# A routed FFN whose tiles are ordered by their rows, with the picks of a token group loaded once a counted number of tiles is scattered

## What is computed

```python
x = _layernorm(x + _L0_attn_ref(x, ...), axis=-1)
x = _layernorm(x + _L0_ffn_ref(x, ...), axis=-1)
```

```python
logits = flat @ router_w.T
probs = jax.nn.softmax(logits.astype(jnp.float32), axis=-1)
topk_p, topk_i = jax.lax.top_k(probs, TOP_K)              # TOP_K = 2, E = 8
topk_w = (topk_p / jnp.maximum(topk_p.sum(-1, keepdims=True), 1e-09)).astype(flat.dtype)
...
for e in range(E):
    out = out + _mlp(flat, w_fc[e], w_proj[e]) * combine[:, e:e + 1]
out = out + _mlp(flat, shared_fc, shared_proj)            # _mlp: square(relu(x @ w_fc.T)) @ w_proj.T
```

## Time and profile before, and how to read it

| | |
|---|---|
| median of 3 runs | 490.98 us (490.75 to 491.0) |
| span of the profiled execution | 498.7 us |
| busy PE, DVE, ACT, POOL | 453.9, 356.7, 354.5, 315.1 us |
| granted TensorE clock, mean | 0.974 |
| first routed load to last `ob` | 327.14 to 470.4 us |
| first pick load to the end | 473.41 to 498.7 us |

### The profile page before, as it was taken

One profiled execution on the slowest core, in us unless ns is written; L12 is line 12 of the kernel. 1 busy time (PEld: TensorE's weight loads), 2 busy tenths in 40 slices (PEclk: granted clock), 3 DMA queues, 4 the chain that ended last, 5 costly groups with the idle time before them and its releaser, 6 DMA issues.

```text
span 498.7 us, 7644 instructions
## 1 busy us (share of the span) xinstructions
PE 453.9 (91%) x2184; PEld 293.6 (59%) x2184; DVE 356.7 (72%) x873; ACT 354.5 (71%) x557; POOL 315.1 (63%) x285
## 2 busy tenths in 40 slices
PE   8997999999999988798898898489999999999983
PEld 5332444444344333455576675389999999899721
DVE  5898999999999999998688964353333333455246
ACT  3989999999999999815455555327667667566537
POOL 4754789999999999845566666604555455555421
PEclk9998999999999999989799999979999999999997
DMA  8031246654343434001111111131222222222095
GB/s 274 8 122 43 86 146 213 216 196 151 130 153 131 151 133 148 3 1 33 39 45 43 45 43 47 46 94 51 72 65 81 71 60 58 60 57 67 11 324 182
DMA packets 41193, 48.56 MB, mean 97 GB/s; under 512 B 5616, under 2 KB 25266, under 8 KB 41152
## 3 DMA queue, kind: packets, MB, share of 16 engines
q1 hardware_dynamic: 35792, 39.07, 23.8%
q0 software_dynamic: 5216, 8.70, 5.6%
q10 hardware_dynamic: 144, 0.31, 0.2%
HBM read 19.17 MB, written 29.11 MB: 97 GB/s over the span
## 4 chain that ended last, share of the span: by engine, by line
PE 40%; POOL 22%; DVE 16%; issue 8%; ACT 7%; DMA 2%; another core or an unknown queue 2%; DVEq 0%; POOLq 0%; SPq 0%; ACTq 0%
POOL memory_feat L495 17%; PE routed_ph L1500 13%; PE routed_po L1513 12%; PE dispatch_sph L998 4%; PE dispatch_spo L1008 3%; POOL memory_feat L503 2%; DVE memory_prod L769 2%; DVE memory_y_raw L778 2%; POOL memory_prod L518 2%; PE memory_nsum L620 1%; ACT finish_xo L1714 1%; PE routed_px L1488 1%; PE dispatch_plr L969 1%; DVE memory_feat L769 1%
## 5 line engine op out<-in xcount | busy, mean ns | idle before, releaser
L495 POOL TENSOR_TENSOR memory_feat<-memory_feat,memory_p_tok 128x1024 f32<-128x1024 f32 x64 | 125.9, 2063 | 17.1 <-ACT memory_feat L390 14.2
L620 PE MATMUL memory_nsum<-memory_feat,tri 128*128 128x512 f32 x256 | 118.1, 604 | 6.3 <-ACT memory_last_rows L403 2.4
L1476 POOL DMA_INDIRECT pick_scratch<-routed_ob,routed_xg x71 | 71.6, 1008 | 75.1 <-DVE routed_ob L1597 56.7
L1192 POOL DMA_INDIRECT table_scratch<-dispatch_xrow,dispatch_slot x64 | 61.9, 967 | 40.9 <-PE dispatch_sph L998 18.9
L620 PEld LDWEIGHTS memory_nsum<-memory_feat,tri 128*128 128x128 f32 x256 | 47.8, 192 | 65.1 <-issue 56.2
L1546 ACT ACTIVATE routed_rel<-routed_ph 128x512 f32<-128x512 f32 x71 | 42.3, 597 | 47.7 <-PE routed_ph L1500 46.7
L1513 PE MATMUL routed_po<-routed_w2c,routed_hid 128*128 128x128 f32 x568 | 71.3, 276 | 1.2 <-DVE routed_ob L1597 0.7
L1500 PE MATMUL routed_ph<-routed_xs,routed_w1c 128*128 128x256 f32 (+1 forms) x368 | 71.1, 337 | 1.2 <-DVE routed_w2c L1583 0.9
L1597 DVE TENSOR_SCALAR routed_ob<-routed_po,routed_xg 128x128 f32<-128x128 f32 x71 | 22.6, 347 | 69.2 <-issue 49.6
L769 DVE TENSOR_TENSOR memory_prod<-memory_nsum,memory_query 128x1024 f32<-128x1024 f32 x58 | 68.8, 1216 | 1.9 <-PE memory_nsum L620 1.8
L1513 PEld LDWEIGHTS routed_po<-routed_w2c,routed_hid 128*128 128x128 f32 x568 | 67.0, 192 | 1.9 <-issue 1.1
(11 more groups left out here) (192 smaller groups left out, 694.6 us busy)
## 6 DMA issues: line engine op xcount, KB each, us to landing
table_scratch<-memory_blank SPq DMA_DIRECT2D x68, 260.0 KB, 2.6
finish_pick<-pick_scratch SPq DMA_DIRECT2D x16, 256.0 KB, 6.0
routed_xg<-table_scratch SPq DMA_DIRECT2D x25, 130.0 KB
w<-w_up SPq DMA_DIRECT2D x9, 256.0 KB, 2.7
w<-w_down SPq DMA_DIRECT2D x9, 256.0 KB, 3.1
x_tok<-x SPq DMA_DIRECT2D x4, 512.0 KB, 3.7
out<-finish_xo SPq DMA_DIRECT2D x7, 256.0 KB, 2.3
routed_xg<-table_scratch SPq DMA_DIRECT2D x21, 65.0 KB
```

The costliest lines, as they stand in the source:

```text
L495: nc.gpsimd.tensor_tensor(v, v, pv, ALU.mult).then_inc(wfeat_done, 1)
L620: last = nc.tensor.matmul(nsum[:, o:o + 512], tri[:], feat[:, i % U, h, q * 512:(q + 1) * 512], start=True, stop=True)
L1192: nc.gpsimd.indirect_dma_start(out=table, in_=xrow[:, r, n, :], in_offset=None, out_offset=bass.IndirectOffsetOnAxis(ap=slot[:, r, n:n + 1 ...
L1476: nc.gpsimd.indirect_dma_start(out=pick_dram, in_=ob[:, u, h, :], in_offset=None, out_offset=bass.IndirectOffsetOnAxis(ap=xg[:, t % XU, h, ...
```

## The change

Five things change.

The order of the routed tiles: candidates are (block k, expert e), k outermost, so all experts' first blocks come first. Partition p = 8 k + e of the chip stands for one candidate, and the list is worked out by small matrix products: `totals` sums the counts of every group (not only the last), DVE marks the candidates that are full (`valid`), PE numbers them with the triangular matrix (`order`), DVE makes a one-hot of the number (`pick_tiles`), PE turns that into lists of experts and starts (`tiles`), and DVE copies them (`list_tiles`); `bases` counts each expert's taken blocks, and the halves go the same way. The numbers of tiles, 25 and 21, stay.

The count: a candidate is needed by a group if the expert's rows up to that group reach into it. `reach` has the tile's number where that is so, PE turns it (`turn_reach`), DVE takes the largest (`far`), and `settle[g]` is that plus 4.

The loads: SP waits no longer for the last scatters but, for each group, for `kept` to reach `settle[g]`, which it loads into a register. As tile t is kept only after the scatter of tile t - 4 has landed, that stands for the scatters of all tiles the group needs. For the last four, POOL raises `kept` when their scatters have landed (`tick`).

The buffers: `pick`, `xo` and the small arrays of `finish` lie where `xrow` and `x_tok` were, or are made earlier (`Late`).

The order on PE in `finish`: `shared(0)` and `shared(1)` come before the routed stage, the rest between the `picks`. The banks are dealt out anew (`BANKS`).

```diff
-        self.seen = sb("seen", [P, 2, E], F32R)
+        self.seen = sb("seen", [P, NG + 1, E], F32R)
...
+class Late:
+    def __init__(self, nc, c, xrow, x_tok):
+        self.pick = xrow[:].rearrange("p r t c -> p (r t c)")[:, 0:2 * NT * D].rearrange("p (r t d) -> p r t d", r=2, t=NT)
...
-            def total():
+            def totals():
                 pe.wait_ge(seen_done, NG + 1)
                 pe.wait_ge(slot_done, NG)
-                nc.tensor.matmul(pr[:, GT * E:], ones_r[:], seen[:, NG % 2], start=True, stop=True).then_inc(total_done, 1)
+                nc.tensor.matmul(p_sum, ones_r[:], seen[:, 1:NG + 1].rearrange("p g e -> p (g e)"), start=True, stop=True
+                                 ).then_inc(total_done, 1)
+            def order(kind):
+                pe.wait_ge(valid_done, kind + 1)
+                nc.tensor.matmul(p_pos[:, kind:kind + 1], tri[:], valid[:, kind:kind + 1], start=True, stop=True
+                                 ).then_inc(order_done, 1)
+            def tiles(kind):
+                pe.wait_ge(chosen_done, kind + 1)
...
+                nc.tensor.matmul(p_tile[:, a:a + n], pair_e, chosen[:, kind, 0:n], start=True, stop=True)
+                nc.tensor.matmul(p_tile[:, TILES + a:TILES + a + n], origin[:] if kind else full_row, chosen[:, kind, 0:n],
+                                 start=True, stop=True).then_inc(tiles_done, 1)
+            def bases():
+                pe.wait_ge(taken_done, 1)
+                nc.tensor.matmul(p_pos[:, 2:3], alike, taken[:], start=True, stop=True).then_inc(base_done, 1)
+            def turn_reach():
+                pe.wait_ge(reach_done, 1)
+                nc.tensor.transpose(p_reach, reach[:, 0], ident[:]).then_inc(reach_turned, 1)
...
+                up(NG - 1, 0)
+                totals()
+                up(NG - 1, 1)
+                down(NG - 2, 0)
+                order(0)
+                down(NG - 2, 1)
+                tiles(0)
+                up(NG - 1, 2)
+                bases()
+                down(NG - 2, 2)
+                order(1)
+                up(NG - 1, 3)
+                tiles(1)
+                down(NG - 2, 3)
+                turn_reach()
                 for t in range(GT):
                     down(NG - 1, t)
...
+            def settle_groups():
+                dve.wait_ge(reach_turned, 1)
+                link(nc.vector.tensor_reduce(far[:], p_reach, AX.X, ALU.max))
+                nc.vector.tensor_scalar(settle[:], far[:], float(U), None, ALU.add).then_inc(settled, 1)
...
                 table_of_tiles()
+                table_of_halves()
                 add_shared(NG - 2)
-                table_of_halves()
+                settle_groups()
                 add_shared(NG - 1)
...
         def sync(sp):
-            for scattered, count in rou.scattered:
-                sp.wait_ge(scattered, count)
+            sp.wait_ge(dis.settled, 1)
             def load(g):
+                tiles = sp.value_load(settle[g:g + 1, 0:1], min_val=U + 1, max_val=TILES + U)
+                sp.wait_ge(rou.kept, tiles)
                 for r in range(2):
...
+        def early_tensor(pe):
+            pe.wait_ge(dis.added, NG - 1)
+            shared(0)
+            pe.wait_ge(dis.settled, 1)
+            shared(1)
...
-            shared(4)
-            shared(7)
-            pe.wait_ge(rou.x_kept, TILES)
-            shared(6)
-            pe.wait_ge(rou.rel_done, rou.banks)
-            for g in range(4):
-                shared(g)
-            pe.wait_ge(rou.kept, TILES)
-            shared(5)
             for n in range(len(PARTS)):
                 if n == 5:
                     pe.wait_ge(act_done, 1)
                     shared(NG)
                 picks(n)
+                if n == 0:
+                    pe.wait_ge(rou.x_kept, TILES)
+                    shared(2)
+                    pe.wait_ge(rou.rel_done, rou.banks)
+                if n + 3 == NG - 1:
+                    pe.wait_ge(rou.kept, TILES)
+                if n + 3 < NG:
+                    shared(n + 3)
...
         def gpsimd(pool):
+            for n, (scattered, count) in enumerate(rou.scattered):
+                pool.wait_ge(scattered, count)
+                nc.gpsimd.memset(tick[:, n:n + 1], 0.0).then_inc(rou.kept, 1)
```

More of the change, by code:

```diff
@@ L91, in build @@
         dis = dispatch(nc, c, early, mem, x_tok, y_all, ident, tri, rows, w_out, routerT, w_up, w_down, w1, w2,
-                       expert, start, table)
+                       expert, start, settle, table)
+        late = Late(nc, c, early.xrow, x_tok)
         rou = routed(nc, c, dis, ident, w1, w2, expert, start, table, pick_dram)
-        fin = finish(nc, c, rou, ident, y_all, eps, warm, pick_dram, out)
+        fin = finish(nc, c, late, dis, rou, ident, y_all, eps, warm, settle, pick_dram, out)
         block = c.enter_context(nc.Block())
@@ L853, in dispatch @@
 def dispatch(nc, outer, early, mem, x_tok, y_all, ident, tri, rows, w_out, routerT, w_up, w_down, w1, w2,
-             expert, start, table):
-    MOST = REGION // ROWS
+             expert, start, settle, table):
     LAST_REDUCES = {2: NT - 2, 3: NT - 1}
@@ L872, in dispatch @@
         ratio, hot, sel, part, seen, base = early.ratio, early.hot, early.sel, early.part, early.seen, early.base
-        hit, spot, slot, steps, fills = early.hit, early.spot, early.slot, early.steps, early.fills
-        one8, whole, used, left, halves = early.one8, early.whole, early.used, early.left, early.halves
-        stride, base0, past, owner, moved = early.stride, early.base0, early.past, early.owner, early.moved
+        hit, spot, slot, mine, total = early.hit, early.spot, early.slot, early.mine, early.total
+        valid, seq, taken, seat = early.valid, early.seq, early.taken, early.seat
+        edge, origin, chosen, reach, far = early.edge, early.origin, early.chosen, early.reach, early.far
         bits = early.bits
@@ L920, in dispatch @@
         token = rows[:, P:P + NT]
+        pair = rows[:, P + NT:]
+        own, full_end, full_at = pair[:, 0:E], pair[:, E:E + 1], pair[:, E + 1:E + 2]
+        pair_e, full_row, half_at, half_row = [pair[:, E + n:E + n + 1] for n in range(2, 6)]
+        alike = pair[:, E + 6:]
         def group(g):
@@ L1050, in rest @@
                 down(0, 3)
-                for g in range(2, NG):
+                for g in range(2, NG - 1):
                     if g + 2 < NG:
@@ L1302, in table_of_tiles, with list_tiles @@
+            def list_tiles(kind):
+                dve.wait_ge(tiles_done, kind + 1)
+                v = slice(FULL, TILES) if kind else slice(0, FULL)
+                nc.vector.tensor_copy(expert[:, v], p_tile[:, v])
+                nc.vector.tensor_scalar(start[:, v], p_tile[:, TILES + v.start:TILES + v.stop], float(P), float(EMPTY),
+                                        ALU.mult, ALU.add).then_inc(tabled, 1)
             def table_of_tiles():
                 dve.wait_ge(total_done, 1)
-                n_e = pr[:, GT * E:]
@@ L1809 @@
     pos = np.arange(L)
[L1810 removed]
+    tabs = np.zeros((P, 2 * P + P + NT + NPAIR), np.float32)
     tabs[:, 0:P] = np.eye(P)
```

197 lines of the change are left out of this document (103 added, 94 removed).

## The result

| | before | after |
|---|---|---|
| median of the runs, first comparison | 490.99 us (490.75 to 491.26) | 487.19 us (485.68 to 487.45) |
| ratio, first comparison | | 0.9919 [0.9898, 0.9940] |
| median, second comparison (17 and 6 runs) | 492.19 us (489.65 to 493.49) | 486.0 us (484.2 to 487.16) |
| ratio, second comparison | | 0.9885 [0.9857, 0.9912] |
| span of the profiled execution | 498.7 us (with pauses) | 485.5 us |

A ratio is a kernel's time over that of the kernel before, run in the same set; the brackets behind it are its 95% interval. The change makes the kernel faster, by 3.8 us in the first comparison and by 6.2 us in the second; 5.3 us were forecast. The first profile of the kernel before holds long pauses.

A forecast was written before the change was run, and what follows sets the result against it. The output stage waits for the last tile's scatter before loading picks; from group 2 ACT is the bound. 490.98 less 5.3 at the end (5.65 gained, 0.3 lost), dispatch stage zero, gives 485.7 us; range 484.4 to 488.6.

The forecast's parts named there:

- The gain at the end: Output stage: early pick loads and PE's new order bring ACT's group 2 at 481.1, not 486.75; 5.3 us net.
- the 0.3 us behind PE: Output stage after group 2: PE keeps 0.14 us a group behind ACT for two groups, 0.3 us lost.
- The loads: Pick loads on SP: from 458.4, behind all `routed_xg` loads, 1.59 us a group, group 7 issued by 471.3.
- The dispatch stage: zero: Before the routed stage: PE gets 3.8 us more work under 6.5 us of cover, so cost zero.
- all six trips: Tile table in the dispatch stage: six PE-DVE trips, each hidden under one FFN step of PE; stall taken as zero.
- The rival in which the trips set the end: Dispatch stage: at 1.7 us stall a trip the routed stage starts 7.3 us later, 493.0 us; chance 0.06.
- the step that counted the new order of the tiles at zero: Routed tiles: SP, POOL and DVE issue the same loads, scatters and copies whichever expert a tile is; zero.
- The first rival: Last routed tiles: early loads slow the last scatters, 1.3 us, 487.0 us; chance 0.16, shared with partly hidden trips.
- the point of 5.9: Last routed tiles: scatter landings of over 5.9 us would make the slower scatters cost time.
- POOL's adds: Output stage: POOL waits for the last scatters (about 473.4); first add wanted at 478.5, so the four stay hidden.
- its counts: Last tile groups 0 to 7 need: new order 8 to 42; old order 25 for group 0, 36 to 42 otherwise.

The follow-up runs named there:

- second comparison: The new kernel, no edit, run again beside the kernel before on another chip than the first four experiments: 486.0 us, ratio 0.9885 [0.9857, 0.9912].
- second profile before: The kernel before, no edit, profiled again, without the long pauses: 491.15 us (one run), span 489.3 us.
- the old order: New kernel with the old tile order and old DVE table, pick loads waiting for constant counts: 485.04 us, ratio 0.9851 [0.9816, 0.9885] to the kernel before.
- all three kernels that had them: 128x512 matmuls added ahead of the routed stage: three to the new kernel 484.33 us, six to the kernel before 490.18, four to the old order 484.07.
- The nine profiles: Kernel before (second profile), new kernel twice, and six edited kernels: late loads, shared matmuls first, old order, three with PE kept busy; spans 481.1 to 491.5 us.

## Why the prediction was right, point by point

**The gain at the end: 5.3 us forecast.** Right in its steps. PE's order sets it as worked out, to 0.01 us at ACT's group 2 (11.24 against 11.25). Against the first profile before, the time from PE's first matmul of the end to the end of the span fell from 28.85 (498.7 - 469.85) to 23.16 us, so by 5.7. ACT did lose the 0.3 us behind PE in groups 3 and 4: its last output comes 8.31 us after that of group 2 (481.89 - 473.58), 7.99 before (494.74 - 486.75). What follows it, DVE's last output and the last store, took 0.35 less, which was not in the sum. Against the second profile before, 6.3: there the loads landed later and the end itself was 0.6 longer.

**The loads.** SP sent the first at 451.7, 11.2 us ahead of the end of DVE's last `ob` at 462.9 (12.0 were forecast, 458.4 against 470.4), and had issued the last at 463.7, 0.8 behind it (forecast 0.9). It waited 1.6 us in all for DVE, and PE for no load.

**The dispatch stage: zero.** The trips and matmuls are hidden, as forecast. From the last group's rank on DVE to PE's last shared `down` it is 12.19 us (314.03 - 301.84) against 11.13 (311.04 - 299.91): 1.06 us more on PE for all six trips (nine small matmuls, with `totals`, where one stood), and 1.88 for the two early shared matmuls, 2.9 in all where 3.8 were forecast, under a wait of 5.20. The rival in which the trips set the end falls. What failed is the step that counted the new order of the tiles at zero, "with no row for a gain" and none for a loss: from the first load to the first `up` it is 4.37 to 4.94 us in the five profiles with the new order, and 4.01 and 4.25 in the two with the old order and no matmuls added, about half a microsecond; in the new order PE waits for the second tile's rows, in the old one for ACT alone.

**Slower scatters.** The first rival's premise was half right: beside the loads a scatter lands in 4.8 us instead of the 2.4 us that is the median over the whole stage. The Trainium skill has on its page "DMA: Bandwidth & Descriptors", Queues, rings and completion order, that each DMA engine goes round its queues packet by packet; the longer landings agree with it, but no run tells that cause from another. The longest landing was 5.2 us, below the point of 5.9 from which it would cost, and no `ob` waited for one. POOL's adds did wait: they begin at 468.15, 5.8 us after PE's first matmul of the end, where the forecast had about 3.6 (473.4 - 469.85), but PE still finds them done. And the last two `up`s of the chain still start 2.00 us apart:

```profile
456.95 1.00 PE routed_ph L1566 x8
...
458.95 1.01 PE routed_ph L1566 x8
```

**The time.** 485.7 against 487.19 and 486.0. By the profiles about half a microsecond is the second tile; the medians are too coarse to show it. The rest of the first comparison's 1.5 us is of the size by which single executions differ through the clock between 210 and 230 us and at the start of the routed stage (first load from 317.34 to 320.22). That in the first comparison the clock was low in most executions of the new kernel fits their mean clock, 0.980 in the three at 487.2 to 487.5 and 0.986 in the one at 485.68; it was not tested on those executions, of which one has a trace. That the forecast comes so close to the second median owes something to luck: there the end gained 6.3 us and not 5.3, and the kernel before was itself slower (492.19) than the 490.98 from which the sum starts.

**What the change's words claim.** The early loads and PE's new order were the gain, as forecast; the prediction did not say that they need the new order of the tiles, but it used it (its counts are 8 to 42 against 25 and 36 to 42) without asking whether SP gets there early enough to profit. The old order shows that it does not.

## What to carry to other kernels

Before building an order of work that lets transfers go early, look when their queue can issue them at all: here SP, held by the loads ahead, came to the picks 11 us before the stage's last `ob`, so late that the plain order of the tiles did as well as the new one. An order of an engine's work that is made for early data is worth something only once the data are early: here the early loads, with two early shared matmuls, took 3.4 us off the end, PE's order with late loads added 2.0, and the two together took off 6.3. And an idle stretch on PE ahead of a long matmul stage (here 5.20 us, or 2.16 and 1.71 us) can cost a second time, in that stage's clock: 1.2 to 2.6 us in the profiles here. A few matmuls into a bank that is free anyway took that back in all three kernels that had them; in the medians 2.0 us for the kernel before, 1.7 or 2.9 for the new one (across sets), and 1.0 for the old order, which is within chance.

## What the runs showed that was not expected

The hole at the start of the routed stage was in view of the first profile as a wait, but its price wasn't: up to 2.5 us through the half clock (6.13 against 3.62 us for 16 matmuls), in both kernels. The nine profiles make the clock the cause: with PE kept busy the granted clock stays at 1.00 from 315 to 330 us and the 16 take 3.62 us in all three kernels, and the stage's time falls by as much. And one small DVE operation of 128x4 numbers, 0.16 us elsewhere, takes 1.09 us in the new kernel while POOL adds two picks:

```profile
469.57 1.09 DVE L1828 SCALAR_TENSOR_TENSOR finish_shift<-finish_mv,finish_rstd 128x4 f32<-128x4 f32 x1
...
470.69 0.81 ACT L1779 ACTIVATE x_tok<-finish_both,finish_shift,finish_rstd 128x128 f32<-128x128 f32 x2 [1.37 <-DVE finish_shift L1828]
```

ACT waits 1.37 us for it. It is so in the kernel before as well (at most 1.03 us there), and the POOL adds that run over it are those from 468.15 shown above; it ends at 470.66, about when the second of the four must (468.15 + 4.94 / 2 = 470.62, an estimate). The Trainium skill, "SBUF — State Buffer", SBUF: two separate sides, has a lock between DVE operations with two inputs in SBUF and POOL's that read SBUF; the times agree with it, but no run here took the POOL adds away.
